# W_func applied before the gather, in a graph network, linear attention and expert kernel

## The reference

```
xn   = layernorm(x)                                   # without gain and bias
h_s  = xn @ W_self.T;   z = xn @ W_func.T
e    = leaky_relu(concat(z[src], z[dst], attr) @ W_att.T)      # one score for each edge
alpha = softmax of e over the edges of one destination
agg  = segment_sum(alpha * z[src], dst)
gnn  = xn + relu(where(deg > 0, h_s + agg, xn))
mix  = linear attention over all nodes: phi(k)^T v and sums, then out, layernorm, ffn (256 -> 1024 -> 256), layernorm
x1   = x + gnn + mix
x2   = x1 + top-2-of-6 experts (three 256x256 products each) of layernorm(x1), chosen by a router 256 -> 128 -> 6
```

## Time and profile before

| what | us |
|---|---|
| median of three runs | 2500.79 |
| profiled execution, its span | 2505.82, 2504.1 |
| first stretch ends (last product of kv) | 260.4 |
| selection starts on PE | 278.86 |
| step loop, first gather to last | 553 to 1896 |
| tail, DVE's first row | 1913.49 |
| experts start on PE | 2086.18 |

### The profile page before, as it was taken

One profiled execution on the slowest core, in us unless ns is written; L12 is line 12 of the kernel. 1 busy time (PEld: TensorE's weight loads), 2 busy tenths in 40 slices (PEclk: granted clock), 3 DMA queues, 4 the chain that ended last, 5 costly groups with the idle time before them and its releaser, 6 DMA issues.

```text
span 2504.1 us, 39252 instructions
## 1 busy us (share of the span) xinstructions
PE 1926.2 (77%) x11133; PEld 1530.7 (61%) x11133; DVE 1556.8 (62%) x3687; ACT 611.9 (24%) x2634; POOL 1668.5 (67%) x1278
## 2 busy tenths in 40 slices
PE   3899577659887777777878767878775778999992
PEld 1444476547766665665666656656654667888882
DVE  4778599877766565566566655656654883226263
ACT  1333388611111111111111111111101323433430
POOL 5554466688888888888888888888884277316164
PEclk8999756569988898898888888888887888999996
DMA  5766788534454444445544444455456455437363
GB/s 155 205 205 189 253 299 294 190 98 133 124 151 127 123 128 123 123 124 134 140 127 123 127 123 123 123 146 132 123 125 182 133 163 153 129 111 199 102 191 96
DMA packets 310586, 378.65 MB, mean 151 GB/s; under 512 B 119740, under 2 KB 263832, under 8 KB 307376
## 3 DMA queue, kind: packets, MB, share of 16 engines
q1 hardware_dynamic: 168932, 234.02, 30.1%
q0 software_dynamic: 141568, 143.66, 23.3%
HBM read 291.57 MB, written 84.76 MB: 150 GB/s over the span
## 4 chain that ended last, share of the span: by engine, by line
PE 34%; POOL 19%; DVE 9%; issue 8%; DMA 5%; ACT 2%; DVEq 2%; SPq 0%; ACTq 0%; POOLq 0%
PE bank L692 32%; POOL wexp L633 17%; DMA wexp<-xn_rows,a_src 4%; PE bank L1018 1%; POOL g_all L679 1%; DVEq L1508 1%; DVE work L1744 1%; DVE work L1749 1%; DVE st L1752 1%; DVE onehot L1668 1%; DVE acc L1680 1%; DVE acc L1766 1%; DVE work L1518 0%; DVE work L1526 0%; SPq L339 0%
## 5 line engine op out<-in xcount | busy, mean ns | idle before, releaser
L633 POOL DMA_INDIRECT wexp<-xn_rows,a_src x900 | 1126.8, 1252 | 274.0 <-issue 258.4
L692 PE MATMUL bank<-wexp,onehot 125*125 125x257 f32 x1800 | 548.7, 459 | 269.9 <-DMA wexp<-xn_rows,a_src 158.8
L692 PEld LDWEIGHTS bank<-wexp,onehot 125*125 125x125 f32 x1800 | 393.5, 228 | 404.2 <-issue 295.1
L1680 DVE TENSOR_TENSOR acc<-bank,acc 125x257 f32 x450 | 190.8, 424 | 419.9 <-PE bank L692 385.0
L1668 DVE TENSOR_SCALAR onehot<-iota_r,a_rel,a_hi 125x125 f32<-125x125 f32 x900 | 289.1, 389 | 0.0
L679 POOL DMA_INDIRECT g_all<-y_d,work x100 | 126.4, 1264 | 218.9 <-DMA y_d<-g_all 117.6
L692 PE MATMUL bank<-g_all 128*128 128x256 f32 x1040 | 238.0, 382 | 8.0 <-DVE g_all L1908 4.6
L692 PEld LDWEIGHTS bank<-g_all 128*128 128x128 f32 x1040 | 193.6, 191 | 33.8 <-issue 6.1
L692 PE MATMUL bank<-work,w_s 128*128 128x250 f32 x800 | 189.0, 378 | 27.9 <-ACT work L1155 27.1
L692 PE MATMUL bank<-s_p,wexp 128*128 128x49 bf16 (+1 forms) x3600 | 143.7, 203 | 62.4 <-DVE wexp L1473 60.6
L692 PEld LDWEIGHTS bank<-work,w_s 128*128 128x128 f32 x800 | 150.4, 191 | 55.7 <-ACT work L1155 35.3
(11 more groups left out here) (269 smaller groups left out, 2739.1 us busy)
## 6 DMA issues: line engine op xcount, KB each, us to landing
wexp<-lr_d SPq DMA_DIRECT2D x75, 750.0 KB
wexp<-in_attr SPq DMA_DIRECT2D x25, 896.0 KB
g_all<-sorted_d SPq DMA_DIRECT2D x65, 256.0 KB
y_d<-g_all SPq DMA_DIRECT2D x65, 256.0 KB, 3.0
wexp<-xn_rows,a_src POOLq DMA_INDIRECT x900, 3.9
sorted_d<-spare SPq DMA_DIRECT2D x48, 256.0 KB, 5.5
sorted_d<-spare SPq DMA_DIRECT2D x24, 384.0 KB, 4.6
work<-xn_rows SPq DMA_DIRECT2D x38, 224.0 KB
```

What stands on the lines that cost most here:

```text
L633: pool.indirect_dma_start(ring[:, 2 * z + k, 0:D], None, xn_rows, bass.IndirectOffsetOnAxis(ap=a_src[:, n // CS, j:j + 1], axis=0)).then_i ...
L692: return pe.matmul(o, l, r, start=first, stop=last_, **kw)
L1680: v.tensor_tensor(to, bank[3 + z % 2][0:R, 0:D + 1], to, ALU.add).then_inc(s("summed"), 1)
```

## The change

`z = xn @ W_func.T` is now made in the first stretch, before the gather, and written to memory as func_rows. `wfuncT_s` has two more columns, which hold u_s, so that a half group's product gives 256 columns of z and both scores. ACT copies z (`func_copy`), DVE copies the two scores into `sc` (`keep_scores`). The banks of func, kv and index products rotate over six; each product waits for the reader of the one six places before it (`bank_read`). The step loop gathers func_rows instead of xn_rows, rows of the same size. In the turn-around, s1 is read from sc as it is, and s2 is made by one transpose of sc, three bf16 parts, and three bf16 products with the one-hot matrix `spread`. The table is 50 x 125. k's bias is three bf16 rows in one product (bk_p); DVE prepares them at the start. In the tail, `agg_turn`, `gnn` and ACT's `agg_copy` are gone, `rows` reads acc, the addition of EPS (L1757) is the bias of ACT's Ln, and `residual` runs on DVE for all groups. W_func is loaded at the start, not in the turn-around.

```
...
-KV_BANKS = (0, 1, 5, 6)
-INDEX_BANKS = [2 + (a + 1) % 2 for a in range(6)]
+ROTATION = (0, 1, 3, 4, 5, 6)
+PRODUCTS = [("blocks", 0, 0)] + [(kind, g, j) for i in range(1, GROUPS + 1) for kind, g, j in
+            [("func", i - 1, 0), ("func", i - 1, 1), ("kv", i - 1, 0), ("kv", i - 1, 1)]
+            + ([("index", i - 8, 0)] if 8 <= i < 14 else [])] + [("spread", k, 0) for k in range(PART)]
+SLOT = {p: n for n, p in enumerate(PRODUCTS)}
+READ_BY = {"func": "scored", "kv": "p1_phi", "index": "a_done", "blocks": "spread"}
 GIN = [(GROUPS + LN - 1 - k) // LN for k in range(LN)]
 XB = 4
...
+            def func_out(g):
+                sp.wait_ge(s("f_done"), 2 * g + 2)
+                load_rows(f"f_out{g % 2}", rows_of(func_rows, g), f_s[g % 2])
+
+            def third_in(q):
+                freed(sp, s("lr_oh"), q - HS + 1)
+                load(f"third_in{(q + 1) % HS}", lr_bc[q % HS], lr_d[q:q + 1].to_broadcast([128, 2 * LROW]))
 
...
-            for g in range(GROUPS - 3, GROUPS):
-                scores_out(g)
-            for k in range(2):
-                sp.wait_ge(s(f"n_s_out{k}"), 32 * ((GROUPS + 1 - k) // 2))
-            sp.wait_ge(s("consts"), CONSTS)
-            load("s1_in", s1_rows[0:HIS - 1, :], s1_d[0:(HIS - 1) * LO, :].rearrange("(h l) a -> h (l a)", l=LO))
-            load("s1_in", s1_rows[HIS - 1:HIS, 0:N - (HIS - 1) * LO], s1_d[(HIS - 1) * LO:N, :].rearrange("n a -> a n"))
-
             sp.wait_ge(s("small_out"), 32)
+            for q in range(HS - 1):
+                sp.wait_ge(s("attr_used"), GROUPS - HS + q + 1)
+                third_in(q)
+            for g in range(GROUPS - 4, GROUPS):
+                func_out(g)
             sp.wait_ge(s("attr_used"), GROUPS)
             load("small_out", ew_d.rearrange("t e -> (t e)").rearrange("(p k) -> p k", p=R), ew_n)
 
-            def third_in(q):
-                freed(sp, s("lr_oh"), q - HS + 1)
-                load(f"third_in{q % HS}", lr_bc[q % HS], lr_d[q:q + 1].to_broadcast([128, 2 * LROW]))
-
-            for q in range(HS):
-                third_in(q)
+            third_in(HS - 1)
...
-            for g in range(PARTS[0]):
-                residual(g)
...
+            def its_bank(kind, g, j):
+                return bank[ROTATION[SLOT[kind, g, j] % len(ROTATION)]]
+
+            def bank_read(kind, g, j):
+
+                n = SLOT[kind, g, j] - len(ROTATION)
+                if n >= 0:
+                    was, g0, j0 = PRODUCTS[n]
+                    pe.wait_ge(s(READ_BY[was]), g0 + 1 if was in ("index", "blocks") else 2 * g0 + j0 + 1)
 
...
             def transposes(g):
                 pe.wait_ge(s("normed"), g + 1)
-                freed(pe, s("columns"), g - 1)
-                if 9 <= g < 15:
-                    pe.wait_ge(s("a_done"), g - 8)
+                freed(pe, s("columns"), g)
                 for c in range(2):
                     for j in range(2):
-                        last = pe.transpose(pt(2 + g % 2)[:, c, j * R:(j + 1) * R], n_x[g % LN][:, j, c * 128:(c + 1) * 128],
+                        last = pe.transpose(pt(2)[:, c, j * R:(j + 1) * R], n_x[g % LN][:, j, c * 128:(c + 1) * 128],
                                             ident[0:R, 0:R])
                 last.then_inc(s("turned"), 1)
 
-            def scores(g):
+            def func(g, j):
                 pe.wait_ge(s("columns"), g + 1)
-                freed(pe, s("n_s"), g)
+                bank_read("func", g, j)
                 for c in range(2):
-                    last = mm(bank[4][0:2, 0:GROUP], u_s[:, c, :], n_xT[g % XB][:, c, :], c == 0, c == 1)
-                last.then_inc(s("n_s_ps"), 1)
+                    last = mm(its_bank("func", g, j)[0:R, 0:D + 2], n_xT[g % XB][:, c, j * R:(j + 1) * R], wfuncT_s[:, c, :],
+                              c == 0, c == 1)
+                last.then_inc(s("func"), 1)
 
             def kv_part(g, j):
-                freed(pe, s("p1_phi"), 2 * (g - 2) + j + 1)
-                to = bank[KV_BANKS[2 * (g % 2) + j]]
+                bank_read("kv", g, j)
+                to = its_bank("kv", g, j)
                 for c in range(2):
                     mm(to[0:R, :], n_xT[g % XB][:, c, j * R:(j + 1) * R], wkv_s[:, c, :], c == 0, False,
                        skip_group_check=True)
-                last = mm(to[0:R, 0:D], ones_row[:, 0:R], bk_r[:], False, True, skip_group_check=True)
+                last = mm(to[0:R, 0:D], ones_p[:, 0:R], bk_p[:, PART, :], False, True, skip_group_check=True)
                 last.then_inc(s("p1_kv"), 1)
...
                     transposes(i)
                 if 0 <= i - 1 < GROUPS:
-                    scores(i - 1)
+                    func(i - 1, 0)
+                    func(i - 1, 1)
                     kv_part(i - 1, 0)
                     kv_part(i - 1, 1)
                 if 8 <= i < 14:
                     index_columns(i - 8)
+                if i == GROUPS + 2:
+                    pe.wait_ge(s("scored"), 2 * GROUPS)
+                    pe.transpose(bank[2][0:BLOCKS, 0:R], sc[:, 1, :], ident[0:R, 0:R]).then_inc(s("look_ps"), 1)
                 if i >= 3:
...
-            pe.wait_ge(s("s1_in"), 32)
-            pe.transpose(bank[6][:, 0:HIS], s1_rows[:], ident[0:HIS, 0:HIS]).then_inc(s("look_ps"), 1)
-            pe.wait_ge(s("s2_in"), 16 * CS)
-            for c in range(CS):
-                last = pe.transpose(bank[0][0:R, c * QS:(c + 1) * QS], s2_rows[:, c * R:(c + 1) * R], ident[0:QS, 0:QS])
+            pe.wait_ge(s("spread"), 1)
+            pe.wait_ge(s("s2_parts"), PART)
+            for k in range(PART):
+                bank_read("spread", k, 0)
+                last = mm(its_bank("spread", k, 0)[0:R, 0:CS * QS], s2_b[:, k, 0:R], spread, True, True)
             last.then_inc(s("look_ps"), 1)
 
...
-            def agg_turn(g):
-                pe.wait_ge(s("columns"), GROUPS + max(0, g - 1))
-                for c in range(2):
-                    for j in range(2):
-                        last = pe.transpose(pt(5 * (g % 2))[:, c, j * R:(j + 1) * R],
-                                            accv[:, 2 * g + j, c * 128:(c + 1) * 128], ident[0:R, 0:R])
-                last.then_inc(s("turned"), 1)
-
-            def gnn(g):
-                pe.wait_ge(s("columns"), GROUPS + g + 1)
-                freed(pe, s("c_r"), 2 * (g - 1))
-                for j in range(2):
-                    for c in range(2):
-                        last = mm(pr_(2 + 2 * (g % 2))[:, j, :], c_aT[g % 2][:, c, j * R:(j + 1) * R], wfuncT_s[:, c, :],
-                                  c == 0, c == 1)
-                last.then_inc(s("c_gnn"), 1)
-
...
+            def func_copy(g, j):
+                act.wait_ge(s("func"), 2 * g + j + 1)
+                if j == 0:
+                    freed(act, s(f"f_out{g % 2}"), 32 * (g // 2))
+                act.activation(f_s[g % 2][:, j], bank[ROTATION[SLOT["func", g, j] % len(ROTATION)]][0:R, 0:D],
+                               ACT.Copy).then_inc(s("f_done"), 1)
...
+            def keep_scores(g):
+
+                for j in range(2):
+                    v.wait_ge(s("f_done"), 2 * g + j + 1)
+                    v.tensor_copy(sc[:, :, 2 * g + j], bank[ROTATION[SLOT["func", g, j] % len(ROTATION)]][0:R, D:D + 2]
+                                  ).then_inc(s("scored"), 1)
...
-                if 9 <= g < 15:
-                    index_columns(g - 9)
+                if 10 <= g < 16:
+                    index_columns(g - 10)
                 if 0 <= g - 1 < GROUPS:
                     p1_edges(g - 1)
                 if g >= 3:
...
-                v.wait_ge(s("c_gnn"), g + 1)
-                if g < PARTS[0]:
-                    v.wait_ge(s("c_res"), g + 1)
-                if g == 0 or g >= PARTS[0]:
-                    o.settle()
+                o.settle()
                 for j in range(2):
-                    v.scalar_tensor_tensor(c_x1[k][:, j], pr_(2 + 2 * k)[:, j], rden[:, 2 * g + j:2 * g + j + 1],
+                    v.scalar_tensor_tensor(c_x1[k][:, j], accv[:, 2 * g + j, 0:D], rden[:, 2 * g + j:2 * g + j + 1],
...
-                    o.did(v.bn_aggr(mv_b[:, 2 * g + j, :], st[:, j, :]))
-                o.settle()
-                v.tensor_scalar(mv_b[:, 2 * g:2 * g + 2, 1], mv_b[:, 2 * g:2 * g + 2, 1], EPS, None,
-                                ALU.add).then_inc(s("var"), 1)
+                    v.bn_aggr(mv_b[:, 2 * g + j, :], st[:, j, :]).then_inc(s("var"), 1)
...
-                if PARTS[0] <= i < GROUPS:
+                if i < GROUPS:
                     residual(i)
...
```

More of the change, by code:

```diff
@@ L264, in build @@
         ring = wexp[0:R, :].rearrange("p (t n) -> p t n", n=D + 1)
-        lr_bc = [wexp[:, k * LPAD:k * LPAD + LROW].bitcast(BF16) for k in range(HS)]
-        lr_oh = [wexp[:, (HS + k) * LPAD:(HS + k) * LPAD + LROW + 2].bitcast(BF16) for k in range(HS)]
+        LR0 = 2 * ZS * (D + 1) - HS * LPAD
+        assert LR0 + LPAD >= ATTRS * CHUNK * ED and LR0 >= HS * LPAD
```

(26 more changed lines are left out.)

140 lines of the change are left out of this document (63 added, 77 removed).

## The result

The changed kernel takes 2528.32 us (median of four runs, 2521.91 to 2532.89), the kernel before 2500.91. The ratio is 1.0109, with a 95% interval from 1.0086 to 1.0131: slower, by 27.4 us or 1.1%. The forecast was 2504.1, with a range from 2487 to 2516. The profiled execution took 2527.8 us, its span 2526.0, 21.9 us longer than the span before.

The account below looks back on a forecast made before the run. POOL was taken to bound the step loop, PE the first stretch, DVE or PE the tail. Terms 5.1 - 5 + 1 + 2.2 = +3.3 on the profiled 2505.8 us gave 2509.1, less 5.0 to the median: 2504.1, range 2487 to 2516.

Parts of the forecast that it names:

- the new wait: First stretch: kv(g) waits for DVE's score copy of g-1, in iteration g+2; room in normal groups, loss where DVE is late.
- After segment_starts ... 0: First stretch, PE's 4.13 us wait: chain longer by the edges, but PE comes 1.2 groups earlier; 0 (-3.5 to +4).
- Normal group, -0.1: First stretch: new product dearer, scores and bias cheaper; -0.1 us a group, 25 times, so -2.5.
- Index groups, 9.2: First stretch, six groups with index columns: 9.2 us each for 9.42, waiting at func; -1.2 in all.
- Group 2, +2.3: First stretch: kv waits for edges behind DVE's slow norm, so the next transposes come 2.3 us later (2 to 4).
- After index_rows ... I take +6: First stretch: PE waits before kv of group 5 for edges and score copies; +6 us (4 to 9).
- Rival 2: First stretch: the wait costs more where DVE's norm meets POOL multiplications, 4 us each; +10, 2514 us; chance 0.25.
- Turn-around, -5: Turn-around: scores skip memory, and the fourth broadcast's chain starts some 3 us earlier; -5 us (-3 to -10).
- about +0.5: End of the first stretch: two broadcasts stand before func_out(21), for whose buffer ACT waits; +0.5 us (0 to 3).
- Selection, +1: Selection: 12 more elements in L1451 for each of 75 slices; +1 us (0 to +3).
- Tail, +2.2: Tail: clock mostly 1.2 GHz, iterations of 5.15 us through PE's chain; +2.2 us (-4 to +6).
- rival 1: Tail: clock stays at 2.4 GHz and DVE sets the pace; -16 instead of +2.2, 2486 us; chance 0.12.

Follow-up runs that it names:

- e1: The changed kernel with func_out of the last four groups sent ahead of the two broadcasts of lr_d: 2529.09 us.
- e3: The changed kernel with four unused products a group on PE in the tail, in the chain before the router's product: 2560.15 us.
- e5: The kernel before, with kv(g) also waiting for DVE's edges of iteration g+2 and the index copies one DVE iteration later: 2529.75 us, ratio 1.0132.
- e7: The changed kernel with all twenty weight loads issued in group 21 of the first stretch: 2529.0 us.
- e8: The changed kernel with four unused products a group on PE in the tail, behind the logits: 2512.98 us.
- e12: The changed kernel with the twenty weight loads issued one to a group, in groups 1 to 20 of the first stretch: 2521.28 us.
- e4_lr_first: The changed kernel with the fourth, fifth and sixth broadcasts of lr_d issued ahead of the twenty weight loads: 2526.52 us.
- e6_keep_out_early: The changed kernel with DVE's score copies one iteration earlier and func_out(g-3) in place of func_out(g-4): 2515.71 us.
- e11_keep_filler: The changed kernel with score copies one iteration earlier, func_out(g-3), and four unused products a group behind the tail's logits: 2495.35 us, ratio 0.9983 to the kernel before.

## Why the prediction was wrong, point by point

The forecast was +3.3 us on the profiled execution and +21.9 were measured. Of the 18.6 between them the first stretch has 15.0 (+19.6 for +4.6), the turn-around with the term beside it 4.6, selection and experts 2.9; tail and step loop give 3.8 back. The mechanism of the loss stood in the prediction, as "the new wait"; what failed is how often it strikes.

- *"After segment_starts ... 0":* this is the step that failed most, with what it left out. PE's wait is 5.10 us for 4.13; that puts group 17 2.6 us later, of which 1.8 are back at group 18. Behind it comes the wait of 5.94 us at 221.19, for which I had no term: +8.4 between groups 18 and 19. DVE has extra work in three iterations, 6, 16 and 18 of the order described for the kernel before, and I reckoned with two of them. How much the third costs depends on how often DVE meets POOL there: with two multiplications in its way PE waited 5.92 to 6.26 us (the changed kernel, e1, e3, e5, e7, e8, e12), with one 1.76 us (e4_lr_first).
- *Normal group, -0.1:* the size is right, -0.13 (7.39 for 7.52). But only about nine of the 24 periods are free of a wait, so it gave 1.2 us and not the 2.5 of the sum: where a wait sets the period, shorter work on PE is lost in the wait.
- *Index groups, 9.2:* right in kind, the wait at func is 1.06 us. The period is 9.35, so -0.4 in all for -1.2.
- *Group 2, +2.3:* it was +3.9 (67.6 for 63.7). The four records of kv after the wait took 3.17 us, for 1.98 at full clock.
- *"After index_rows ... I take +6":* about right. The delay grows from 4.4 us at group 6 to 13.4 at group 7 and is 11.2 at group 8, so +6.8 up to the group after, where the 2 us come back as the working says.
- Rival 2 named this mechanism (norm beside POOL, 4 us each, from 10.6 us on). e5_before_wait shows the wait, put into the kernel before, to cost 17.7 us up to group 24, and e6_keep_out_early, which takes it away, gives 10.1 of the 19.6 back (12.6 us by the medians). Its price of +10 in all was too low. It named only the norm; in index_rows and `edges_in_block` other instructions are held up, too.
- *Turn-around, -5:* it was 0. The scores' way is 8.5 us shorter, but the fourth broadcast sets the end, and the weight loads ahead of it start as long after group 24 as before (14.7 us for 14.8), and not 3 us sooner; the loss of the first stretch comes through whole. ACT waited 8.49 us for func_out's buffer, and eight transfers of func_rows kept SP to 280.3. I had both down as "about +0.5".
- *Selection, +1:* from the wait's end to the gather it is 190.2 for 187.7, +2.5.
- *Tail, +2.2:* it was +0.9, with an iteration of 5.11 us for 5.15 and the clock at 0.50. That the clock falls, and what it costs, stood as forecast; e8_pe_filler gives the price of it, 15.3 us for the forecast's 18.2 between its own case and rival 1. That the sum came so near is luck in part. Its working to route 0 does not add up: three iterations of 4.2 to 4.9 and ten of 5.15 from 1916.4 on end between 1980.5 and 1982.6, not at 1985.1, which is -1 to -3 and not +1.5. Measured was +0.3 to route 0, +2.1 from there to route 1 (for +2.9) and -1.5 behind it (for -0.7). Stretches at 2.4 GHz, for which 1.5 was taken off, there were none in the two stretches shown above.
- *Step loop, experts, last stores, 0:* the experts and stores took 1.4 us more. The step loop came out 2.5 us shorter in this profile. From the first gather to the tail's first row it takes 1434.0 before, 1431.4 here and 1434.9 in e11_keep_filler; what makes the 3 us is open.

Left open: the first stretch differs between executions of the same program. The changed kernel, e1, e3, e4 and e8 have the same instructions up to group 24, and its transposes start at 266.4, 267.5, 268.8, 258.3 and 268.2. In e4_lr_first, the early one, the step from group 18 to 19 took 9.4 us (16.0 in the changed kernel):

```profile
206.60 1.72 DVE L1406 SCALAR_TENSOR_TENSOR acc<-acc,onehot 75x1500 f32<-75x1500 f32 x1
206.96 5.75 POOL L584 TENSOR_TENSOR wexp<-wexp,awe 125x2048 f32<-125x2048 f32 x1 [12.62 <-DMA wexp<-in_attr]
...
209.30 3.88 DVE L1294 TENSOR_SCALAR work<-work,mv,rstd 125x256 f32<-125x256 f32 x2
...
215.49 1.98 PE L673 MATMUL bank<-work 128*125 128x512 f32 x4 [1.76 <-DVE sc L1365]
```

That explains 6.6 us of that profile. Whether it also explains the spread of the runs (2516.69 to 2531.01 in e4, 2518.9 to 2532.5 in e5_before_wait, but 2492.72 to 2506.69 in seventeen runs of the kernel before, too) is not shown, and a mark read from a single profile of the first stretch is sure only to about 10 us. The comparisons above therefore go by the medians where they can.

## What to carry to other kernels

When buffers are reassigned, write down for each wait which iteration of the other engine it now asks for; one more can be free in a normal group and cost at every place where that engine has extra work, so count all of these. Work taken from an engine can cost clock: here four products and four transposes a group less on PE, with the residual more on DVE, left the tail as long as it was (+0.9 us), and four useless ones in PE's idle time, off the chain, took 15 us away, while on the chain they cost 32. Where a chain waits for the last of a row of transfers, moving others within the row did not shorten it here; spreading them over an earlier stretch did, at the price of a part of the gain there.
